# Output projection of attention: half each in places 1 and 2 of the next quad, with a new order on VectorE

## The reference

```python
def attn(x, w_q, w_kv, w_out, b_out, scale):      # 16 heads of 64
    q, k, v = split_heads(x @ w_q), split_heads(...), split_heads(...)   # of x @ w_kv
    q = l2norm(q) * exp(scale)
    k = l2norm(k)
    attn = softmax(q @ k.T)                       # 512 x 512 per head
    out = merge_heads(attn @ v)                   # 512 x 1024
    return out @ w_out + b_out

def ffn(x, ...):                                  # weights are -1, 0 or 1 with a scale per row
    h = silu(x @ w1.T * s1) * (x @ w2.T * s2)     # 1024 wide
    h = gelu(h @ h1.T * t1)
    h = gelu(h @ h2.T * t2)
    return h @ w3.T * s3

x = x + layernorm(attn(layernorm(x)))
x = x + layernorm(ffn(layernorm(x)))
```

## Time and profile before

| | us |
|---|---|
| median of 3 runs | 1826.78 (1825.06 to 1828.6) |
| the profiled execution | 1824.77 |
| its span, first to last instruction | 1823.0 |
| TensorE matmuls busy | 1716.2 |
| VectorE busy | 1191.4 |
| ScalarE busy | 1007.2 |
| GpSimd busy | 488.5 |
| mean granted TensorE clock | 0.987 of 2.4 GHz |

### The profile page before, as it was taken

One profiled execution on the slowest core, in us unless ns is written; L12 is line 12 of the kernel. 1 busy time (PEld: TensorE's weight loads), 2 busy tenths in 40 slices (PEclk: granted clock), 3 DMA queues, 4 the chain that ended last, 5 costly groups with the idle time before them and its releaser, 6 DMA issues.

```text
span 1823.0 us, 24702 instructions
## 1 busy us (share of the span) xinstructions
PE 1716.2 (94%) x8608; PEld 1430.9 (78%) x8608; DVE 1191.4 (65%) x2026; ACT 1007.2 (55%) x1350; POOL 488.5 (27%) x563
## 2 busy tenths in 40 slices
PE   7999999989989999998999997999999999999998
PEld 6777777777778777777778775788888888888887
DVE  6777877877777777777778775554454545454454
ACT  6767767767776776776667666413232332313231
POOL 5433533543443443443452451000000000000000
PEclk9999999999999999999999999999999999999999
DMA  5446456455455545546454655310000000000000
GB/s 157 96 126 162 100 133 155 107 134 130 115 124 131 128 112 132 139 100 145 111 122 120 160 133 146 115 68 1 24 1 24 12 12 24 1 23 1 24 1 24
DMA packets 76700, 162.75 MB, mean 89 GB/s; under 512 B 28256, under 2 KB 28640, under 8 KB 76576
## 3 DMA queue, kind: packets, MB, share of 16 engines
q1 hardware_dynamic: 67216, 127.98, 29.2%
q10 hardware_dynamic: 8352, 29.50, 5.3%
q0 software_dynamic: 1008, 3.67, 0.5%
HBM read 68.97 MB, written 20.19 MB: 49 GB/s over the span
## 4 chain that ended last, share of the span: by engine, by line
PE 51%; DVE 16%; issue 11%; DMA 7%; POOL 6%; SPq 5%; ACT 3%; DVEq 0%; ACTq 0%; POOLq 0%
PE pair L1250 12%; PE pair L1251 12%; PE bank L1187 5%; PE bank L1173 5%; DMA Dp<-work 5%; PE bank L1098 4%; DVE Pl L789 3%; DVE work L805 3%; PE pair L1240 3%; PE pair L1241 3%; POOL rs L417 2%; PE pair L1154 2%; PE pair L1155 2%; PE bank L1267 2%; PE bank L1268 2%
## 5 line engine op out<-in xcount | busy, mean ns | idle before, releaser
L561 ACT ACTIVATE P<-pair,sh 128x1024 f32<-128x1024 f32 x256 | 286.0, 1117 | 255.6 <-PE pair L1155 212.7
L1250 PE MATMUL pair<-hh,f 128*128 128x512 f32 x1024 | 399.3, 390 | 0.7 <-DVE hl L903 0.2
L1251 PE MATMUL pair<-hl,f 128*128 128x512 f32 x1024 | 398.5, 389 | 0.0
L1173 PE MATMUL bank<-Ph,V 128*128 128x512 f32 x1024 | 367.5, 400 | 30.0 <-ACT work L572 30.0
L789 DVE TENSOR_TENSOR Pl<-P,Ph 128x1024 fp32r<-128x1024 f32 x256 | 320.9, 1254 | 12.5 <-ACT Ph L566 12.5
L611 ACT ACTIVATE hr<-pair,ct 128x512 f32<-128x512 f32 x128 | 88.3, 690 | 357.5 <-PE pair L1251 357.5
L1098 PE MATMUL bank<-w,xh 128*128 128x512 f32 (+1 forms) x1016 | 280.3, 338 | 3.1 <-DVE turned L783 3.1
L566 ACT ACTIVATE Ph<-P 128x1024 fp32r<-128x1024 f32 x256 | 271.5, 1061 | 8.1
L1173 PEld LDWEIGHTS bank<-Ph,V 128*128 128x128 f32 x1024 | 194.4, 190 | 85.5 <-ACT Ph L566 31.4
L1250 PEld LDWEIGHTS pair<-hh,f 128*128 128x128 f32 x1024 | 192.2, 188 | 43.8 <-DVE hl L903 3.5
L1251 PEld LDWEIGHTS pair<-hl,f 128*128 128x128 f32 x1024 | 192.2, 188 | 39.7
(11 more groups left out here) (126 smaller groups left out, 2697.4 us busy)
## 6 DMA issues: line engine op xcount, KB each, us to landing
stack<-turned SPq DMA_DIRECT2D x127, 384.0 KB, 4.2
stack<-turned SPq DMA_DIRECT2D x127, 256.0 KB, 4.8
work<-rows SPq DMA_DIRECT2D x128, 128.0 KB, 3.1
raw<-in_h ACTq DMA_DIRECT2D x16, 512.0 KB, 3.8
xr<-in_h ACTq DMA_DIRECT2D x16, 512.0 KB, 3.7
f<-raw ACTq DMA_DIRECT2D x12, 512.0 KB, 5.5
f<-raw SPq DMA_DIRECT2D x10, 512.0 KB, 8.7
xr<-in_x SPq DMA_DIRECT2D x8, 512.0 KB, 5.9
```

What stands on the lines that cost most here:

```text
L561: e.activation(M.P[:, i % 2, :], M.SB[i % 2][:, :], ACT.Exp, bias=M.sh[:, h:h + 1]).then_inc(S["exp"])
L1173: d = e.matmul(M.OB[:, :], v, p[:, u % 4, j * 512:(j + 1) * 512], start=jt == 0 and m == 0, stop=jt == 3 and m == 2)
L1250: e.matmul(ps, w, M.hh[src][:, k, :].bitcast(to), start=k == 0, stop=False)
L1251: d = e.matmul(ps, w, M.hl[src][:, k, :].bitcast(to), start=False, stop=k == KH - 1)
```

## The change

The output projection of a quad is no longer 24 matmuls in place 7, but half in place 1 and half in place 2 of the following quad (`part_of` for `quad_of`). VectorE takes in each place P's low half of the place before first, then the additions, low parts of turned pairs, sums and low parts of values that belong to the place before, then the scaling of tiles from two places before, then normalising. Every pair is normalised in place 3 or 7 and inverted in place 0 or 4, the last pairs too. The even pair is turned in place 4, not 5, and both its halves are stacked in place 6. GpSimd's and ScalarE's loops, the places of the layer norms, the transposes of x (both in place 21 of a sequence), the weight looks and loads are shifted to go with it, and `bank_plan` holds longer for each user.

The core of the diff:

```diff
@@ -76,14 +76,14 @@
 
 def pair_of(i):
 
-    n = 2 * (i // 8) + {0: 1, 5: 2}.get(i % 8, NP)
+    n = 2 * (i // 8) + {0: 1, 4: 2}.get(i % 8, NP)
     return n if n < NP else None
 
 
-def quad_of(i):
-
-    n = (i - 15) // 8
-    return n if i % 8 == 7 and 0 <= n < NQ else None
+def part_of(i):
+
+    Q, r = (i - 17) // 8, i % 8
+    return (Q, r - 1) if r in (1, 2) and 0 <= Q < NQ else None
 
 
 def bank_plan():
@@ -99,18 +99,19 @@
             order.append((("Tk", pair_of(i)), i))
             if i:
                 order.append((("Tq", pair_of(i)), i))
-        if quad_of(i) is not None:
-            order += [(("y", 2 * quad_of(i)), i), (("y", 2 * quad_of(i) + 1), i)]
-        if b < B and i % 32 in (19, 20):
-            order.append((("x", 2 * (b + 1) + i % 32 - 19), i))
+        if part_of(i) is not None:
+            order.append((("y", 2 * part_of(i)[0] + part_of(i)[1]), i))
+        if b < B and i % 32 == 21:
+            order += [(("x", 2 * (b + 1) + k), i) for k in range(2)]
         if i == FLAG_AT:
             order.append((("flag", 0), i))
     order += [(("x3", n), SLOTS + n) for n in range(2, 2 * B)]
+    held = {"qk": 2.4, "v": 1.9, "Tk": 1.5, "Tq": 1.8, "x": 1.7, "y": 1.6, "flag": 1.5, "x3": 1}
     plan, last, free = {}, {}, {0: -3, 1: -3, 2: -3}
     for n, (user, i) in enumerate(order):
         bank = user[1] % 2 if user[0] == "x3" else min(free, key=free.get)
         plan[user] = bank, last.get(bank)
-        last[bank], free[bank] = user, i + n / len(order) + {"qk": 1, "x": 1.5 if i >= 0 else 0}.get(user[0], 0)
+        last[bank], free[bank] = user, i + n / len(order) + (held[user[0]] if i >= 0 else 1 if user[0] == "qk" else 0)
     return plan
 
 
@@ -201,25 +202,25 @@
 F3, F4, F5 = 4, 12, 20
 
 
-LOADS = (223, 226, 227, 231, 234, 235, 239, 242, 243, 247, 250, 251)
-
-LOOKS = (16,) + tuple(32 * b + r for b in range(7) for r in (21, 24, 29))
-COUNTS = (19,) + tuple(32 * b + r for b in range(7) for r in (23, 27, 31))
-
-
-
-RAWS = tuple(8 * q for q in range(1, 28) if q < 8 or q % 4 != 3)
+LOADS = tuple(8 * q + r for q in range(28, 32) for r in (0, 1, 4))
+
+LOOKS = (12,) + tuple(32 * b + r for b in range(7) for r in (24, 28, 33))
+COUNTS = (17,) + tuple(32 * b + r for b in range(7) for r in (26, 30, 36))
+
+
+
+RAWS = tuple(8 * q + 1 for q in range(1, 28) if q == 4 or q % 4)
 
 
 
 
 
 def invert_slot(n):
-    return NU - 3 if n == NP - 3 else 4 * n + 8
+    return 4 * n + 8
 
 
 def normal_slot(n):
-    return {NP - 4: NU - 3, NP - 3: NU + 1}.get(n, 4 * n + 11 - n % 2)
+    return 4 * n + 11
 
 
 def low_slot(n):
@@ -351,27 +352,23 @@
         i32_, pb = i % 32, i // 32 - 1
         for n in pairs(invert_slot, i):
             store_rec(n)
-        for n in pairs(invert_slot, i - 1):
-            if n % 2:
-                spread_rec(n)
         if i % 2 and 0 <= i // 2 - 2 < NG:
             take_sums(i // 2 - 2)
         for n in pairs(invert_slot, i - 1):
-            if n % 2 == 0:
-                spread_rec(n)
-        if i % 8 == 6 and pair_of(i - 1) is not None:
-            stack(pair_of(i - 1), 1)
-        if 0 <= pb < B - 1 and i32_ == 16:
+            spread_rec(n)
+        if r == 1 and pair_of(i - 1) is not None:
+            stack(pair_of(i - 1), 0)
+        if r in (2, 6) and pair_of(i - 2) is not None:
+            if r == 6:
+                stack(pair_of(i - 2), 0)
+            stack(pair_of(i - 2), 1)
+        if 0 <= pb < B - 1 and i32_ == 18:
             store_x1(pb)
-        if pair_of(i) is not None:
-            stack(pair_of(i), 0)
-        if i % 8 == 2 and pair_of(i - 2) is not None:
-            stack(pair_of(i - 2), 1)
         if i == 3:
             load_x(1)
         if b + 2 <= B and i32_ == 31:
             load_x(b + 2)
-        if 0 <= pb and i32_ == 6:
+        if 0 <= pb and i32_ == 9:
             load_xr(pb)
     load_xv(0)
     load_xv(1)
@@ -478,20 +475,20 @@
     for i in range(SLOTS):
         g, c, b, r, live = slot(i)
         i32_, pb = i % 32, i // 32 - 1
-        if b < B and i32_ == 5:
-            norm_root(b + 1)
+        for u in tiles_of(i - 1) if i else []:
+            head_root(u)
         for n in pairs(normal_slot, i):
             o_high(n)
-        if b < B and i32_ in (5, 12):
-            for t in (0, 1) if i32_ == 5 else (2, 3):
+        if b < B and i32_ == 9:
+            norm_root(b + 1)
+        if 0 <= pb < B - 1 and i32_ == 14:
+            out_root(pb)
+        if b < B and i32_ in (12, 14):
+            for t in (0, 1) if i32_ == 12 else (2, 3):
                 ln1b(b + 1, t)
-        if 0 <= pb < B - 1 and i32_ == 12:
-            for t in range(NT):
+        if 0 <= pb < B - 1 and i32_ in (15, 17):
+            for t in (0, 1) if i32_ == 15 else (2, 3):
                 add_x(pb, t)
-        for u in tiles_of(i):
-            head_root(u)
-        if 0 <= pb < B - 1 and i32_ == 11:
-            out_root(pb)
     out_root(B - 1)
     for b in range(B):
         for n in range(3):
@@ -818,7 +815,8 @@
         if Q % 4 == 0:
             q.wait_ge("bb", 16)
             q.wait_ge("wl", WPOS[7])
-            q.wait_ge("x1r", NT * (Q // 4))
+            if Q:
+                q.wait_ge("x1r", NT * (Q // 4 - 1) + 2 * half + 2)
         q.wait_ge("yb", n - 1)
         e.tensor_tensor(y, M.G[PLAN["y", n][0]][:, :].rearrange("p (a b) -> p a b", a=2),
                         y if Q % 4 else M.bb[:, :].unsqueeze(1).to_broadcast([128, 2, 256]), ALU.add).then_inc(S["yb"])
@@ -958,68 +956,46 @@
     for i in range(NU + 1):
         g, c, b, r, live = slot(i)
         i32_, pb, n = i % 32, i // 32 - 1, i // 4 + 1
-        if b < B and i32_ == 21:
+        if b < B and i32_ == 22:
             x_low(b + 1, 0)
-        for n in pairs(invert_slot, i):
-            if r == 4:
-                invert(n)
+            x_low(b + 1, 1)
         if 0 <= i - 1 < NU:
             p_low(i - 1)
+        if i and part_of(i - 1) is not None and i < BRANCH_AT:
+            add_part(*part_of(i - 1))
+        if i and pair_of(i - 1) is not None:
+            turn_low(pair_of(i - 1), 1)
+            turn_low(pair_of(i - 1), 0)
+        for u in tiles_of(i - 1) if i else []:
+            head_sums(u)
+        if i and values_of(i - 1) is not None:
+            v_low(values_of(i - 1))
         for n in pairs(invert_slot, i):
-            if r == 5:
-                invert(n)
-        if i == NU - 7:
-            turn_low(NP - 1, 1)
-            turn_low(NP - 1, 0)
+            invert(n)
+        for u in tiles_of(i - 2) if i > 1 else []:
+            head_scale(u)
+        for n in pairs(low_slot, i):
+            o_low(n)
+        for n in pairs(normal_slot, i):
+            normal(n)
         if i < 3:
             split_w(4 + i)
         if i in (5, 6):
             split_wo(i - 3)
-        for n in pairs(low_slot, i):
-            o_low(n)
-        for n in pairs(normal_slot, i):
-            if n % 2:
-                normal(n)
         if 0 <= pb < B - 1:
-            for t in {8: (0, 1), 10: (2,), 11: (3,)}.get(i32_, ()):
+            for t in {10: (0, 1), 12: (2,), 13: (3,)}.get(i32_, ()):
                 finish(pb, t)
-            if i32_ == 12:
-                for t in range(NT):
-                    out_scale(pb, t)
+            for t in {14: (0, 1), 16: (2, 3)}.get(i32_, ()):
+                out_scale(pb, t)
         if b < B:
-            for t in {3: (0,), 4: (1, 2, 3)}.get(i32_, ()):
+            for t in {5: (0, 1), 6: (2,), 8: (3,)}.get(i32_, ()):
                 ln1(b + 1, t)
-            if i32_ == 21:
-                x_low(b + 1, 1)
-        for u in tiles_of(i):
-            head_sums(u)
-        if values_of(i) is not None:
-            v_low(values_of(i))
-        if i and pair_of(i) is not None and i != NU - 8:
-            turn_low(pair_of(i), 1)
-            turn_low(pair_of(i), 0)
-        if i == 1:
-            turn_low(1, 1)
-            turn_low(1, 0)
-        for u in tiles_of(i - 1) if i else []:
-            head_scale(u)
-        for n in pairs(normal_slot, i):
-            if n % 2 == 0:
-                normal(n)
-        for n in pairs(invert_slot, i):
-            if r == 0:
-                invert(n)
-        if quad_of(i) is not None and i < BRANCH_AT:
-            add_part(quad_of(i), 0)
-            add_part(quad_of(i), 1)
         if i in COUNTS:
             count_piece(COUNTS.index(i))
-        if i == FLAG_AT - 4:
+        if i == FLAG_AT - 3:
             count_all()
         if i == FLAG_AT + 1:
             flag()
-    normal(NP - 3)
-    o_low(NP - 3)
     for b in range(B):
         for n in range(3):
             for m in range(KH):
@@ -1291,11 +1267,11 @@
         if pair_of(i) is not None:
             turn(pair_of(i), 1)
             turn(pair_of(i), 0)
-        if quad_of(i) is not None and i < BRANCH_AT:
-            outp(quad_of(i), 0)
-            outp(quad_of(i), 1)
-        if i < NU and i % 32 in (19, 20):
-            x_turn(i // 32 + 1, i % 32 - 19)
```

(5 more changed lines are left out.)

10 lines of the change are left out of this document (5 added, 5 removed).

## The result

The changed kernel takes 1732.37 us (median of 4 runs, 1729.8 to 1734.88) beside 1825.92 us for the kernel before in the same comparison (1824.59 to 1828.6): ratio 0.9486, 95% interval 0.9467 to 0.9505. That is 93.6 us off; 82 were predicted, and a time of 1743. The profiled execution took 1734.88 us, with a span of 1733.1 (before: 1823.0), so the two traces differ by 89.9 us.

What follows compares the result with a forecast made beforehand. TensorE, busy 94% of the span, was taken as the bound, losing 11.9 us per sequence to waits and slow clock. Gains of 95 + 9 less 22 of new waits gave 82 us off 1824.8: 1743 us, range 1717 to 1792.

Steps and rivals of the forecast that it cites:

- the bare sequence: TensorE's sequence without waits: 128.0 us against 139.94 measured, so 11.9 us per sequence, 95 us in all, would go.
- The low half: Output projection: its wait for VectorE's low half, 49.7 us in all, goes, and with it the clock steps.
- The tail: End of the kernel: pairs 60 and 61 done in places 251 and 255 bring 9 us.
- (a): Even pair turned in place 4: second key load lands 7.3 us into place 5, wanted at 8.3, slack 1.0 us.
- the slower rival: Place 0 waits for the even pair's keys in every quad: 1830 us, up to 1876; chance 6%.
- (b): Reciprocal ahead of the products in place 0: waits for sums, 0.25 us per quad, 8 us in all.
- (c): Banks in places 2 and 3, freed by VectorE's scaling: 0.1 us per quad, 3 us in all.
- (d): Once per sequence, weight look in place 28 just ahead of the stacking: about 1 us each, 7 us in all.
- (e): Tail: weight loads in places 0, 1 and 4 of the last four quads, keys late again, 4 us.
- GpSimd beside VectorE: Place 0: P's low half first delays GpSimd's products, 0.9 us more on a chain with 0.7 us slack.
- All hand-overs hold: Rival: nothing new is late at the median landings, only some 5 us come back, 1726 us; chance 24%.
- A new wait in each quad: Rival: each quad gets a new wait of 1.5 to 2.5 us, 1788 us; chance 22%.

Runs made afterwards that it cites:

- e6: The changed kernel with weight looks and the last quads' weight loads moved so no 512 KB transfer starts just ahead of the even pair's stacking: 1718.71 us, ratio 0.9411.
- e2: The kernel before, its output projection taking the high half in place of the low one and waiting only for the high: 1765.51 us, ratio 0.9683.
- e10: The kernel before with idle transposes filling TensorE's waits in every place 7 of a quad: 1813.23 us, ratio 0.9934.
- e7: The changed kernel with the last pairs inverted and normalised where the kernel before did it: 1734.46 us, ratio 0.9506.
- e9: The changed kernel with the even pair turned in place 5 and its stacking ahead of the load of sums in SP's program: 1806.45 us, ratio 0.989.
- e3: The changed kernel with the even pair turned in place 5 and its keys stacked in place 7: 1880.91 us, ratio 1.0323.
- e4: The changed kernel with VectorE's and GpSimd's products taken in the place that makes them, P's low half still first: 1804.95 us, ratio 0.9905.
- e5: The changed kernel with both halves of the output projection in place 1: 1775.79 us, ratio 0.9722.

## Why the prediction was right, step by step

**The bound and the bare sequence** were right. 139.94 us against a bare 128.0 was called a loss of 11.9 per sequence; the third sequence now takes 128.54, and 127.64 in e6. The product 8 x 11.9 held in sum, not in each: the first sequence ends 6.1 us earlier than before, and the next six are shorter by 9.8, 11.4, 11.7, 10.8, 15.0 and 11.6. The bare length came from adding cadences of the chain of waits, and it was within 0.4 us. The first two sequences are longer after, 133.3 and 130.2 us at clocks of 0.97 and 0.99, with waits for keys of 3.34 and 2.67 us, so the sign "clock 1.00 through the attention" did not hold there; the next five take 128.2 to 129.1. In e6 the second takes 127.7.

**The low half** went as the working had it, and e2 shows that with the clock behind it it was the larger part (58 of 94). **Bank 3** fell to 1.3 us for the reason given: ScalarE's copy had waited for VectorE's product 24 times, 15.0 us (L572), and after it has no such wait left. **The clock** was right in kind: 12 us by e10 alone, and 19.5 us of matmul time between the two traces.

**The tail** was put at 9 us. From place 240 to 255 TensorE takes 58.19 us after and took 62.86 before, though after has one projection (24 matmuls, 2.9 us) more in that stretch: 7.6 us like for like. The size was near, the reason mostly not: the pairs' new places were to bring it, and e7 without them loses 2.4 us there. Where the other 5 come from is not shown; that 9 came near 7.6 is in part luck. The statement on the longest wait (under 3 us) was wrong. The trace of after there:

```profile
1046.31 0.77 PE L1130 MATMUL pair<-stack 128*128 128x512 f32 x1 [3.50 <-issue]
...
1049.30 0.20 DVE L794 RECIPROCAL Rp<-Dp 128x8 f32<-128x8 f32 x1 [4.38 <-DMA Dp<-work]
...
1057.75 0.47 PE L1149 MATMUL bank<-Ph,V 128*128 128x512 f32 x1 [1.66 <-DVE Pl L786]
```

The 5.93 us of the earlier trace rows are gone, but the keys are late (3.50), and the sums (4.38), and P's low half once (1.66). In e6, which moves the weight loads of places 1 and 4, the same stretch takes 52.96 us at a clock of 1.00.

**(a), the even pair in place 4.** Right, and nearly to the tenth: in a quiet quad the second stacking load is issued 2.56 us into place 5 and lands 4.7 later, at 7.26 where 7.3 was said. Place 0 wants it at 8.4, so the slack is 1.2 us for the 1.0 that was worked out, and e9 and e3 show what lies behind it: 74 us for a pair turned one place later, and with SP's order on top the slower rival's far end, 1881 us (1876 was worked out).

**(b), the reciprocal ahead of the products in place 0,** is the term that was mis-sized. 8 us were put in; TensorE's waits for the scaled tile (`PE bank L1105 <- DVE qk L757`) are 2.6 us in 4 goes, and none stands in most quads. Only two of them, 0.27 and 0.78 us, stand behind a reciprocal that VectorE waited for; the longest, 1.35 us, is a late inverse root from GpSimd. 0.25 us was taken in each of 31 quads, between a median of 0 and a far end of 3, as if every quad had some of the long landing; but VectorE stood still before a reciprocal in 17 of 64 pairs, 14 times for under 1.6 us, and the median's 0 holds in the others.

**(c)** was about right in size and wrong in place: 3 us put in; no wait stands in places 2 and 3, but a projection tile in place 17 of a sequence takes 1.63 us for 1.39, behind VectorE's low half of a turned pair, some 2 us over all sequences. **(d) and (e)** were right in cause and sum: 11 us put in; 12.2 us of waits for keys stand after, seven between sequences or behind the first look (8.7 us) and one in the tail (3.5). They stand at a first score of a place 0, the sign that was given for (a) too; that (a) is not the cause is shown by e6, which moves just these DMAs and gets 14 back. Here the rule of the Trainium skill (DMA: Bandwidth & Descriptors, Issuing engines are not separate DMA queues) that DMAs of all issuers run on the same 16 engines and interleave agrees with the traces: the load takes 4.7 us alone and 6.6 beside a look from another issuer's queue, and 4.6 again in e6 with the look moved.

**GpSimd beside VectorE.** The rule of the Trainium skill (GPSIMD Engine Reference, Key points) that GpSimd contends with VectorE instructions of two SBUF inputs was read as more delay under the new order. The maximum of the earlier trace rows became shorter in the mean (467 to 377 ns, x124), as it now runs beside P's low half 10 times and not 31; the last step of the same chain became longer (229 to 554 ns). From the start of the first to the end of the third the chain went from 2.59 to 2.91 us in the mean. So it grew by 0.3 us, not by 0.9, and of TensorE's 2.6 us under (b) one wait of 1.35 can be put down to it.

The sum: 104 us of gain less 22 gave 1743; the profiled run is 14 us above what the 104 alone would give (1720.8). 12.2 + 2.6 of waits account for it. Of the 8 us that the 22 were too large by, 5.4 are (b) and some 1 is (c); (d) and (e) were 1 too small, and 2 to 3 us are not named.

**The rivals.** All hand-overs hold (1726) was nearly as close, and is what e6 realises. A new wait in each quad (1788) did not come, but three small departures from the change bring it: e4, e5 and e9 are at 1776 to 1806, each with one wait of 1 to 2 us per quad. What I did not see is how much of the gain hangs on the parts that I had taken to be aids.

**Left open:** how bank 3's 28.7 us and the clock share the 36 us that e2 did not take; no run removed bank 3's wait alone. And e5's two halves were tried in place 1 only, with VectorE's additions behind its scaling, so whether another bank or another place for the additions would do as well is not known.

## What to carry to other kernels

Add up a bare period from the cadences of the chain of waits, and compare it with the window: the difference is what a reordering can give, and it is reached only when every hand-over moves with it (here undoing one of three parts cost 43 to 153 us, beside a gain of 94). When a consumer's wait is gone, look at the queue that issues the next critical DMA: what stands ahead of it in program order, and which large transfer from another queue starts just before it. Put the cost of a rare long landing on the quads that have its cause, not on all.

## What the runs showed of the hardware

- The granted clock fell behind a wait that was left: filling place 15 alone moved the slow stretch to place 7 of the same sequence (8.14 to 9.62 us, at 0.82 for 1.00) and gained nothing; filling all gained 12 us. A wait's price is thus not its own length alone, nor is it got back one by one.
- The first stacking load of 256 KB of an even pair lands 4.7 us after issue in quiet quads and 6.6 behind a 512 KB transfer that another engine issued 2.3 us earlier; the pair's second such load, issued 2.0 to 2.4 us later, takes 5.6 to 5.8 in quiet quads. The longest of all 127 is 10.1.
- Four DMAs in a row on SP's queue do not issue at one rate: 0.49 and 0.65 us for the first two, then 1.67 and 1.42 us (after, from 409.93). The fourth goes out 2.4 us after the second.
- GpSimd and VectorE got in each other's way one instruction at a time, and the one that began second was the one that took longer. GpSimd's cast of 128x512 beside P's low half, first from the trace of before, then from e4's:

```profile
638.19 0.61 POOL L441 CAST nh<-work 128x512 fp32r<-128x512 f32 x1 [3.51 <-DVE work L805]
638.27 1.60 DVE L789 TENSOR_TENSOR Pl<-P,Ph 128x1024 fp32r<-128x1024 f32 x1
...
460.19 1.23 DVE L786 TENSOR_TENSOR Pl<-P,Ph 128x1024 fp32r<-128x1024 f32 x1
...
460.22 1.66 POOL L438 CAST nh<-work 128x512 fp32r<-128x512 f32 x1 [4.92 <-DVE work L802]
```

Where the cast began first (19 times in before) it took 0.61 us and P's low half 1.6 in the mean; where P's low half began first (60 times in e4) that took 1.23 and the cast 1.66. So the mean of the cast is 0.66 us after and 1.60 in e4, which differ only in the order of these two engines' work, while the chain of inverse roots takes 2.91 and 2.54. One order is better for one of them and worse for the other. Beside VectorE's scaling, which reads a bank of PSUM, the maximum of 128x8 stayed at 0.24 us (61 times in before); beside P's low half it took 1.14 (31 times).
